# A third key and value buffer, earlier routing, 32-row-outermost stores, and expert outputs one pair later in a fused attention and expert kernel

## What is computed

```
xn = layernorm(x)
s = attention(xn)                         # keys and values for all tokens
probs = softmax(xn @ gate_w + gate_b, over tokens)
vals, idx = top_k(probs, 8)               # for each batch and expert
merged = sum_k xn[idx] * vals             # one row for each batch and expert
o = gelu(merged @ w1) @ w2
g = silu(scatter_add(o * vals at idx))
x = x + s * g
... layer 1
```

## Time and profile before

| | us |
|---|---|
| median of 3 runs | 2973.69 |
| profiled execution | 2973.5 |
| its span, first to last instruction | 2971.8 |
| first sweep, to the first key matmul | 0 to 85 |
| key loop, to TensorE's last matmul in it | 85 to 313 |
| from there to attention's first matmul | 313 to 373 |
| attention | 373 to 961 |
| scatter stage | 961 to 1011 |
| layer 1 | 1011 to 2972 |
| mean granted TensorE clock | 0.941 |

### The profile page before, as it was taken

One profiled execution on the slowest core, in us unless ns is written; L12 is line 12 of the kernel. 1 busy time (PEld: TensorE's weight loads), 2 busy tenths in 40 slices (PEclk: granted clock), 3 DMA queues, 4 the chain that ended last, 5 costly groups with the idle time before them and its releaser, 6 DMA issues. The chain is left out here.

```text
span 2971.8 us, 39206 instructions
## 1 busy us (share of the span) xinstructions
PE 2569.5 (86%) x13290; PEld 1485.8 (50%) x13290; DVE 2307.5 (78%) x2777; ACT 2025.9 (68%) x3268; POOL 2068.6 (70%) x650
## 2 busy tenths in 40 slices
PE   5876288888887669999999999999999999999977
PEld 2333133333333435665655655656656556566455
DVE  6576476656562359899899898998998998989985
ACT  3221145556565369788798888897887988888864
POOL 0454441000000159999999999999999999999996
PEclk9998579999899779999999999999999999999989
DMA  8334398767650232132231320321322313213210
GB/s 274 102 105 126 102 264 205 199 165 197 169 166 10 93 121 96 40 122 77 74 122 44 107 112 25 122 100 49 122 72 79 122 37 114 102 35 121 93 51 8
DMA packets 133884, 322.69 MB, mean 109 GB/s; under 512 B 13233, under 2 KB 89009, under 8 KB 117314
## 3 DMA queue, kind: packets, MB, share of 16 engines
q1 hardware_dynamic: 113186, 248.84, 27.4%
q0 software_dynamic: 19200, 70.73, 7.2%
q10 hardware_dynamic: 1312, 0.66, 0.1%
HBM read 277.12 MB, written 43.13 MB: 108 GB/s over the span
## 5 line engine op out<-in xcount | busy, mean ns | idle before, releaser
L1449 DVE TENSOR_TENSOR_SCAN l_st<-l_p_a,l_hl,l_st 128x512 f32<-128x512 f32 x768 | 932.5, 1266 | 106.1 <-ACT l_p_a L1708 95.2
L1630 POOL TENSOR_TENSOR l_st<-l_st,l_cs 128x2048 f32<-128x2048 f32 x192 | 871.5, 4567 | 0.0
L1708 ACT ACTIVATE l_p_a<-l_dt,lw_a_neg 128x512 f32<-128x512 f32 x1024 | 664.8, 680 | 45.2 <-DVE keep_xg L1449 37.0
L1622 POOL TENSOR_TENSOR l_st<-l_bs,l_dtu 128x2048 f32<-128x2048 f32 x128 | 584.4, 4566 | 29.7 <-PE l_p_y L1979 27.5
L1979 PEld LDWEIGHTS l_p_y<-keep_ident,l_st 128*128 128x128 f32 x3072 | 354.1, 144 | 143.7 <-POOL l_st L1630 77.0
L1979 PE MATMUL l_p_y<-keep_ident,l_st 128*128 128x128 f32 x3072 | 384.3, 281 | 48.0 <-POOL l_st L1630 47.8
L969 ACT ACTIVATE a_pr<-a_p_s 128x512 f32<-128x512 f32 x512 | 284.5, 596 | 161.6 <-PE a_p_s L1035 143.7
L893 DVE TENSOR_REDUCE a_mpart<-a_p_m 128x1 f32<-128x512 f32 x512 | 315.2, 683 | 97.7 <-PE a_p_m L1000 95.8
L1449 DVE TENSOR_TENSOR_SCAN keep_xg<-l_p_a,l_hl,keep_xg 128x512 f32<-128x512 f32 x256 | 314.8, 1267 | 1.6
L1630 POOL TENSOR_TENSOR keep_xg<-keep_xg,l_cs 128x2048 f32<-128x2048 f32 x64 | 292.5, 4570 | 2.0 <-ACT l_hl L1713 2.0
L1035 PE MATMUL a_p_s<-a_qst,kx 99*128 99x256 bf16 x1024 | 204.2, 289 | 74.1 <-ACT a_pr L969 55.1
(11 more groups left out here) (225 smaller groups left out, 3920.7 us busy)
## 6 DMA issues: line engine op xcount, KB each, us to landing
a_w<-in_w_dram POOLq DMA_DIRECT2D x64, 1024.0 KB, 11.9
l_bs<-s_bc SPq DMA_DIRECT2D x64, 1024.0 KB, 4.7
l_cs<-s_bc SPq DMA_DIRECT2D x64, 1024.0 KB, 4.8
keep_share<-s_x SPq DMA_DIRECT2D x32, 512.0 KB, 4.9
s_kp<-t_kp SPq DMA_DIRECT2D x96, 128.0 KB
kx<-s_kp SPq DMA_DIRECT2D x16, 768.0 KB, 11.1
s_vp<-t_vo SPq DMA_DIRECT2D x16, 544.0 KB
a_vg<-s_vp SPq DMA_DIRECT2D x16, 544.0 KB, 11.9
```

The source lines that it names most:

```text
L1449: eng.tensor_tensor_scan(st[k % NG][:, n, :], p_a[:, n, :], st[k % NG][:, n, :], hl[:, k, n:n + 1], ALU.mult, ALU.add).then_inc(scan_ok, 1)
L1622: eng.tensor_tensor(st[n][:, :, :], bs[:, 4 * n:4 * n + 4, :], dtu[(k // NG) % 2][:, :].unsqueeze(1).broadcast_to([P, NG, TT]), ALU.mult). ...
L1630: eng.tensor_tensor(st[n][:, :, :], st[n][:, :, :], cs[:, 4 * n:4 * n + 4, :], ALU.mult).then_inc(cm_ok, 1)
L1708: eng.activation(p_a[:, n, :], dt[c % 2][:, :], ACT.Exp, scale=a_neg[:, c, m:m + 1]).then_inc(dA_ok, 1)
```

## The change

1. **Stores.** The scratch layouts of keys and queries are reordered, so that each store's DRAM pattern has 32 rows of 4 pieces where it had 4 blocks of 32. The loads of them become six DMAs of 16 rows where there were three of 48, 32 and 16.
2. **Buffers.** kp and vo have three buffers, in memory that attention uses for w2 later; k32 has two. The end of the stage no longer waits for the key stores.
3. **x1.** It is no longer stored tile by tile, but copied from x in DRAM by eight 1 MB DMAs during attention.
4. **Routing.** Its pieces move to earlier tiles; `share_of`, `rank_of` and `place` leave the preparation and become `one_choice`, half a choice's columns at a time, once in each attention step. The queries are split at tiles 10 to 12, stored at 13 and 14, and those of the first two steps are loaded before the stage ends.
5. **Attention** is written out in full instead of looping over b; `outputs` of a quad runs two steps later, after the second score of chunk 1, beside the next gelu; VectorE copies its result and GpSimd stores it. The rows of ones are loaded, not set by GpSimd (four memsets of 6.9 us each before).
6. **Scatter** gathers xg again, since rows of ranks stand in its memory meanwhile.

```diff
         def store_queries(eng, part):
 
             eng.wait_ge(qsplit, (1, 3, 4)[part])
-            for g in (2 * part, 2 * part + 1):
+            for eo in two:
                 for b in range(B):
-                    eng.dma_start(scr["qp"].rearrange("b a (q z) t -> b q a z t", q=6)[b, g],
-                                  qp[:, g // 2, g % 2, b * SB:(b + 1) * SB]).then_inc(q_out_g if part == 2 else q_out, 16)
+                    eng.dma_start(scr["qp"][b, part, :, eo].rearrange("a (h t) -> a h t", h=4),
+                                  qp[:, part, eo, b * SB:(b + 1) * SB]).then_inc(q_out, 16)
...
-                        eng.wait_ge(x_out[t % 4], t // 4 * 16)
...
-                    eng.wait_ge(x_in[t % 4], t // 4 * 16 + 16)
-                    eng.dma_start(scr["x1"][t * TT:(t + 1) * TT, :].rearrange("(a p) d -> p a d", p=P), xb[t % 4]).then_inc(x_out[t % 4], 16)
                     if 1 <= t < NT - 3:
...
                 def keys_out(r):
-                    p = r % 2
+                    p = r % 3
                     eng.wait_ge(kp_ok, r + 1)
                     for g in range(6):
-                        part, eo = divmod(g, 2)
-                        dst = scr["kp"][r * HG * 48:(r + 1) * HG * 48, :].rearrange(
-                            "(a q z) t -> a q (z t)", a=HG, q=6)[:, g, :].rearrange("a (z t) -> a z t", t=TT)
-                        eng.dma_start(dst, kp[p][:, part, eo, :]).then_inc(stored[p], 16)
+                        eng.dma_start(scr["kp"].rearrange("(r c a e) (h t) -> r c e a h t", c=3, a=HG * 8, e=2, h=4)[r, g // 2, g % 2],
+                                      kp[p][:, g // 2, g % 2, :]).then_inc(stored[p], 16)
                     eng.wait_ge(vo_ok, r + 1)
                     eng.dma_start(scr["vp"][r * HG:(r + 1) * HG, :, :].rearrange("a p n -> p a n"),
                                   vo[p][:, :, :, :, :].rearrange("p a b c d -> p a (b c d)")).then_inc(stored[p], 16)
 
...
-                    eng.wait_ge(side, 16)
-                    eng.dma_start(rowb, scr["rows"].rearrange("p k -> (p k)").partition_broadcast(P)).then_inc(side, 16)
-                    eng.dma_start(rankb, ins["rank"].rearrange("p k -> (p k)").partition_broadcast(P)).then_inc(side, 16)
...
                 def group_keys(hg):
-                    for p in two:
-                        eng.wait_ge(stored[p], 2 * STORES)
+                    for j in three:
+                        eng.wait_ge(stored[j], (2, 1, 1)[j] * STORES)
                     eng.wait_ge(kr_ok, 4 * hg + 8)
...
+                    for i, part in enumerate((0, 1, 2, 0, 1, 0)):
+                        eng.dma_start(kst[hg][16 * i:16 * i + 16, :, :, :].rearrange("r c z t -> r c (z t)"),
+                                      scr["kp"].rearrange("(b c k a r) n -> b k a r c n", b=B, c=NC, k=3, a=HG)[0, part, hg, :, :, :])\
                            .then_inc(side, 16)
+                    eng.dma_start(ones[hg], ins["ones"]).then_inc(side, 16)
+
+                def group_queries():
+                    eng.wait_ge(q_out, 16 * 6 * B)
+                    for hg in two:
+                        for i, part in enumerate((0, 0, 0, 1, 1, 2)):
+                            eng.dma_start(q0[hg][16 * i:16 * i + 16, :, :].rearrange("r z t -> r (z t)"),
+                                          scr["qp"][0, part, hg * 8:hg * 8 + 8].rearrange("j e n -> (j e) n")).then_inc(side, 16)
 
                 for t in range(NT + 2):
                     if t >= 2:
                         keys_out(t - 2)
...
+                    if t == 13:
+                        store_queries(eng, 0)
...
+                    if t == NT:
+                        group_queries()
+                eng.wait_ge(side, 16 * (1 + 2 * 7 + 2 * 6))
...
-                    wait(eng, r1_ok, t)
+                    wait(eng, r1_ok, t - 1)
...
-                    p = t % 2
+                    p = t % 3
                     eng.wait_ge(v_ok, t + 1)
-                    wait(eng, stored[p], t // 2 * STORES)
+                    wait(eng, stored[p], t // 3 * STORES)
...
-                    if t == 5:
                         merge()
-                    if t == 6:
-                        for k in range(3, 6):
-                            share_of(k)
-                    if t == 7:
-                        for k in range(6, 8):
-                            share_of(k)
...
+                    if t in (8, 9):
+                        query_turn(t - 8)
...
-                for p in two:
-                    i = eng.memset(vo[p][:, :, :, :, HD:VW], 1.0)
+                eng.memset(share[:, :], 0.0)
+                for j in three:
+                    i = eng.memset(vo[j][:, :, :, :, HD:VW], 1.0)
...
-            for hg in range(HG):
-                step(hg, 0, hg)
-            with eng.Fori(1, B) as b:
-                for hg in range(HG):
-                    step(b * HG + hg, b, hg)
+            for g in range(G):
+                step(g, g // HG, g % HG)
...
+                    if hg == 0 and b:
+                        all_stored(eng)
+                    kp = scr["kp"].rearrange("(b c k a r) n -> b k a r c n", b=B, c=NC, k=3, a=HG)
+                    for i, part in () if early(b, hg) else enumerate((0, 1, 2, 0, 1, 0)):
...
+                    if 2 <= g < HG:
+                        eng.dma_start(kx[(hg + 1) % HG][R:RM, :].bitcast(I32), ins["ones"]).then_inc(ones_ok, 16)
...
+                    if g == HG - 1:
+                        for dst, src in ((rowb[:, :], scr["rows"].rearrange("p k -> (p k)").partition_broadcast(P)),
+                                         (rankb[:, :], ins["rank"].rearrange("p k -> (p k)").partition_broadcast(P)),
+                                         (rank[:, :], ins["rank"])):
+                            eng.dma_start(dst, src).then_inc(consts, 16)
+                    if hg % 2:
+                        half = bass.ds(b * S + hg // 2 * (S // 2), S // 2)
+                        eng.dma_start(scr["x1"][half, :].rearrange("(p a) d -> p (a d)", p=P),
+                                      ins["x"][half, :].rearrange("(p a) d -> p (a d)", p=P)).then_inc(x1_out, 16)
...
-                for h in range(HG):
-                    eng.memset(kst[h][R:RM, :, :, :], 1.0).then_inc(ones_ok, 1)
...
+                def one_choice(g, b, hg):
+
+                    k = b * 2 + hg // 2
+                    wait(eng, shares, 6 * g)
+                    eng.tensor_copy(col[:, 0:1], gf[:, bass.ds(k, 1)])
+                    eng.tensor_copy(col[:, 1:2], vals[:, bass.ds(k, 1)]).then_inc(shares, 1)
+                    for h in two:
+                        cols = slice(h * TT, h * TT + TT)
+                        eng.wait_ge(shares, 6 * g + 2 * h + 1)
+                        if hg % 2 == 0:
+                            eng.tensor_scalar(found[:, :], rowb[:, cols], col[:, 0:1], col[:, 1:2], ALU.is_equal, ALU.mult).then_inc(shares, 1)
+                            eng.wait_ge(shares, 6 * g + 2 * h + 2)
+                            eng.tensor_tensor(share[:, cols], share[:, cols], found[:, :], ALU.add).then_inc(shares, 1)
+                        else:
+                            eng.scalar_tensor_tensor(found[:, :], rowb[:, cols], col[:, 0:1], rankb[:, cols], ALU.is_equal, ALU.mult)\
+                               .then_inc(shares, 1)
+                            eng.wait_ge(shares, 6 * g + 2 * h + 2)
+                            eng.tensor_reduce(part[:, h:h + 1], found[:, :], AX.X, ALU.max).then_inc(shares, 1)
+                    eng.wait_ge(shares, 6 * g + 5)
+                    if hg % 2:
+                        eng.tensor_tensor(top[:, bass.ds(k, 1)], part[:, 0:1], part[:, 1:2], ALU.max).then_inc(shares, 1)
+                    else:
+                        eng.memset(part[:, :], 0.0).then_inc(shares, 1)
...
+                        if i == 8 and hg % 2 == 0 and g > 2:
+                            experts_out(g // 2 - 2)
                         eng.tensor_reduce(mpart[p][:, i // NC, i % NC:i % NC + 1], p_m[i % 4][:, :], AX.X, ALU.max)\
...
+                def experts_out(q):
+                    eng.wait_ge(o_ok, q + 1)
+                    wait(eng, eo_out, q * 64)
+                    eng.tensor_copy(eo[:, :], p_e[:, 0:D]).then_inc(eo_ok, 1)
...
+                        if g == 1:
+                            eng.wait_ge(consts, 16 * 4)
...
-                    eng.wait_ge(o_ok, q + 1)
-                    wait(eng, eo_out, q * 64)
-                    eng.activation(eo[:, :], p_e[:, 0:D], ACT.Copy).then_inc(eo_ok, 1)
-                    eng.wait_ge(eo_ok, q + 1)
-                    for j in range(4):
-                        eng.dma_start(scr["oe"][:, bass.ds(q * 4 + j, 1), :].rearrange("b a n -> b (a n)"),
-                                      eo[32 * j:32 * j + B, :]).then_inc(eo_out, 16)
+                    eng.activation(hT[q % 2][:, :, :, :], hT[q % 2][:, :, :, :], ACT.Gelu).then_inc(hg_ok, 1)
...
```

(33 more changed lines are left out.)

363 lines of the change are left out of this document (169 added, 194 removed).

## The result

| | before | after |
|---|---|---|
| median, us | 2974.74 (4 runs) | 2854.81 (4 runs, 2849.87 to 2858.88) |
| profiled execution, us | 2973.5 | 2858.9 |
| start to first key matmul | 84.6 | 79.4 |
| key loop to TensorE's last matmul | 228.6 | 181.5 |
| gap to attention's first matmul | 59.6 | 24.6 |

The ratio to before is 0.9597 (95% interval 0.9578 to 0.9615): 120 us faster, with 2810 forecast and 2780 to 2862 given as the range. The profiled execution lies 49 us above the forecast. The stages show where: 3.8 in the first sweep, 11.9 in the key loop, nothing in the gap, 22 in the intervals of attention, 8.2 behind the last closing copy, 3.1 in layer 1.

The account below looks back on a forecast made before the run. It took store waits to bound the key loop, with no engine full, and waits and lower clock to slow the gap and attention. Terms: -9 - 59 - 35 - 64 + 3 = -164, from 2973.5 to 2810 us; range 2780 to 2862.

Parts of the forecast that it names:

- one of its own signs: Whole forecast: it is wrong if the key loop stays above 188 us or attention above 548.
- First sweep: Start to 85 us: x1 stores gone, buffer free at normalisation, part of the DMA waits stays; -9 us, bounds 4 and 13.
- Stores and buffers in the loop: Key loop: wider-spread stores and a third buffer leave it bound by its own work, 170 us; -59 (-40 to -68).
- rival 4: Key stores still run on few engines, only the third buffer helps: 20 us in loop, 8 in gap, 2838; chance 0.08.
- The gap: Between key loop and attention: no query stores, memsets or wait for key stores; 25 us remain, -35 (-25 to -42).
- Odd and even intervals: Attention: outputs beside gelu, ScalarE freed, half of one_choice shows; odd 32.5 us, even +3 over eight; attention sum -64.
- The step that failed: SP's queue in attention: loads behind x1 copies are needed a step or two later, so hidden; 2 us extra issues hidden.
- Rival 3: Attention: x1 copies delay the next loads in SP's queue, every second step waits; 3034 at 90 us a copy; chance 0.02.
- The last step: End of attention: loses its tail of outputs on ScalarE but keeps the matmuls; -4 us.
- the scatter stage: After attention: gathering again by eight indirect DMAs ends at 977 against first use at 974.27; +3 us (0 to +6).
- The stores as no bound of the loop: Key loop: stores weren't its only bound, a chain across four engines sets 12 us a tile; 2835; chance 0.17.
- VectorE as attention's bound: Attention: VectorE's maxima and one_choice bound it, odd intervals 37 us, even 32, 41 more; 2851; chance 0.13.

Follow-up runs that it names:

- both_old: The changed kernel with two key and value buffers instead of three and key stores back at 4 blocks of 32 rows: 2934.25 us, ratio 0.9857.
- old_stores: The changed kernel with only the key stores back at 4 blocks of 32 rows, loads matched, three buffers kept: 2897.33 us, ratio 0.9733.
- outputs_after2: The changed kernel with broadcasts issued early, and expert outputs after the weighted values following chunk 2 instead of beside gelu: 2853.64 us, against 2830.02 without the move.
- consts_first: The changed kernel with the broadcasts of rows and ranks and the rank table issued with step 0's loads instead of step 3's: 2830.02 us, ratio 0.9508.

## Why the prediction was right or wrong

The forecast was 164 us, the profiled executions differ by 115. By one of its own signs the forecast was wrong, though the time fell inside the range: it set 188 us for the loop (181.5 measured) and 548 for attention, and attention runs from 285.47 us to VectorE's last copy in it, 557.7 us in all:

```profile
842.75 0.42 DVE L925 COPY keep_accT<-a_p_acc 128x256 f32<-128x256 f32 x1 [11.96 <-PE a_p_acc L1042]
```

Step by step:

- *First sweep:* -9 forecast, -5.2 measured. Mis-sized: waits of 15.6 us stayed, not 12, since the gap behind the key weights shrank from 11.24 to 9.85 only.
- *Stores and buffers in the loop:* -59 forecast, -47.1. The mechanism was right and is shown by both_old: stores and too few buffers together made the wait of 49.2 us, and the plateau at 0.2 follows the store's shape. The stores take about 4 us a tile, not 2 to 3. Two sizes were wrong. I counted 17 us of matmuls above 16 x 8.6 and 15 us of waits; it is 159.6 - 137.6 = 22 of matmuls and 22 of waits. So the places where routing and queries hold tiles up cost 22 us, not 15. And rival 4 priced the old shape at 20 us in the loop and 8 in the gap, where old_stores has 1.8 and 27.5: in the loop the third buffer is worth more, the shape works in the gap.
- *The gap:* -35 forecast, -35.1, made up nearly as supposed: about 11 us of the last tile's chain (TensorE ends at 260.9, GpSimd's last part at 271.8), then SP's issues, twelve query loads ahead of the last six key stores. Two readings were off without effect on the sum. All 33 issues at 0.66 would be 22 us, not 17 (20 of them stood behind the chain). And of the four memsets only the first could hold TensorE up: GpSimd starts them at 365.78 us, and TensorE starts at 372.84.
- *Odd and even intervals:* 32.5 and 30.7 forecast, 32.1 and 29.9 measured. That 32.1 is so near is luck in part. The 40.0 us that I started from was the longest odd interval without a loop's return; four others took 36.0 to 39.0. And the place of the outputs was priced at 5.4 us (2.70 of wait, 2.7 of clock), where outputs_after2 shows 2.4 to 3.4. How much the freed ScalarE brings by itself (2.24 and 1.3) no run separates. In one_choice I took half of 2.9 us; the share step has 2.8 us in the trace and 1.6 to 1.9 of it showed; the even intervals, ahead of which the rank step stands, did not grow.
- *The step that failed* is the one on loads in SP's queue during attention. The prediction said of the loads in SP's queue that they "are needed a step or two later; hidden", and looked only at keys and at the copies of x1. It did not follow the wait `consts`, which the diff adds ahead of L941 for all four loads, to where they stand in the queue: +22.8 us in one interval, a fifth of what the change brought, and an edit of one line returns it (31.0 us in consts_first). Rival 3 had the mechanism (loads behind other traffic in SP's queue) but named the wrong load and priced it per step.
- *The last step:* -4 forecast for it and +3 for the scatter stage, +7.2 measured, for both together. The outputs of two quads now fall into the last step with one buffer of second weights, so the last quad waits 7.21 us for 4 MB and then runs at the lower clock (6.43 us for 3.64). The gather cost less than priced, 1.05 us of wait at its first use:

```profile
859.48 0.42 DVE L1197 TENSOR_TENSOR c_xo<-c_s,c_xg 128x256 f32<-128x256 f32 x1 [1.05 <-DMA c_xg<-in_x_dram,keep_g]
```

- *Rivals.* The stores as no bound of the loop: false, the loop went from 233.6 to 181.5 by shape and third buffer together, and seven of its fifteen tile distances are 8.6 to 9.2 us, so there is no chain of 12 us. VectorE as attention's bound: false for even intervals, in part true for the share step. The copies of x1 (eight, landing in 13.6 to 33.0 us): never waited for. Unchanged store width: false.
- Layer 1 took 3.1 us more in after's profile. In the other profiles it is 1958.5 to 1963.4 us; I take it for the spread of single executions.

That the measured time fell inside the range owes something to luck: the loss of 22.8 us and the one of 8 us were in none of the cases with a price; the range had room for them because rivals 1, 2 and 4, which did not come true in the main, had widened it.

## What to carry to other kernels

When a wait is moved or added, list every DMA that its semaphore counts and find each in its queue, with what is issued ahead of it; a wait for "constants" is as late as the last of them. Two edits that cure the same wait don't add: price them together, and look for the second place (here the end of the loop, where nothing hides the stores) in which they differ. Small work on an engine costs time by its place, not by its size: 2.8 us of VectorE behind a wait cost an odd interval 1.9 us more than ahead of it.

## What the runs showed of the hardware

A key store of 128 KB ran at a busy share of 0.2 and 80 to 98 GB/s with 4 blocks outermost and at 0.4 to 0.7 and 146 to 262 GB/s with 32 rows outermost, the same bytes in the same runs of 1 KB. While the DMA engines were busy throughout, the issue itself was slow: six key loads took 3.31 us to issue at 288 us and 18.72 us at 295 (that SP's queue was full is my reading). In the attention of after, written out, TensorE has no wait like the 5.72 us of "issue" at the loop's return; its only wait of this name is the 7.21 us for the last weights. The Trainium skill ("Runtime: NRT & Kernel Launch", section "Instruction fetch mechanics") has a taken branch out of the fetched window stall the engine, and straight code prefetched; these rows agree, and no run here changes the loop alone.
